# Gate of a graph network: at three steps TensorE folds a product tile alone, and GpSimd's addition is left out

## The reference, cut to what matters

```python
def _gate(h, q, Wg, bg, Wq, bq):           # h: 8 x 32 nodes x 768, q: 8 x 64 x 768
    hg = einsum('bnf,gf->bng', h3, Wg[:, :F])
    qg = einsum('blf,gf->blg', q, Wg[:, F:]) + bg
    attn = sigmoid(hg[:, :, None, :] + qg[:, None, :, :])
    qi = einsum('bnlf,blf->bnf', attn, q)
    alpha = sigmoid(einsum('bnf,gf->bng', h3, Wq[:, :F]) + einsum('bnf,gf->bng', qi, Wq[:, F:]) + bq)
    return (alpha * tanh(qi) + (1.0 - alpha) * h3).reshape(B * N, F)
```

## Time and profile before

| | |
|---|---|
| median of 3 runs | 822.61 us (822.32 to 822.70) |
| profiled execution | 822.72 us, span 820.9 us |
| PE busy | 773.7 us (94%) |
| DVE busy | 606.1 us (74%) |
| POOL busy | 514.2 us (63%) |
| ACT busy | 424.9 us (52%) |
| L590 POOL, first additions | 94 in 223.0 us, mean 2394 ns |
| L1424 PE, identity products | 464 records in 58.9 us |
| L1974 DVE, gate products | 96 in 217.7 us, mean 2279 ns |

### The profile page before, as it was taken

One profiled execution on the slowest core, in us unless ns is written; L12 is line 12 of the kernel. 1 busy time (PEld: TensorE's weight loads), 2 busy tenths in 40 slices (PEclk: granted clock), 3 DMA queues, 4 the chain that ended last, 5 costly groups with the idle time before them and its releaser, 6 DMA issues.

```text
span 820.9 us, 10574 instructions
## 1 busy us (share of the span) xinstructions
PE 773.7 (94%) x4196; PEld 641.8 (78%) x4196; DVE 606.1 (74%) x664; ACT 424.9 (52%) x507; POOL 514.2 (63%) x219
## 2 busy tenths in 40 slices
PE   7999999999988999988888889999999999998998
PEld 4669986776645699667655548999999999975897
DVE  8966239999999641888999996865696488565454
ACT  6524447677674342666676735444443454253742
POOL 0625609999999273499999964870685177805500
PEclk9999999999999999999999999999999999999999
DMA  9037525345332474260063327556356545350001
GB/s 365 31 78 233 163 88 157 86 147 155 115 116 77 123 231 146 67 180 12 26 231 116 108 85 268 194 192 221 103 177 204 181 137 210 116 231 0 2 1 39
DMA packets 24409, 111.01 MB, mean 135 GB/s; under 512 B 3620, under 2 KB 6180, under 8 KB 23976
## 3 DMA queue, kind: packets, MB, share of 16 engines
q1 hardware_dynamic: 23240, 104.24, 39.3%
q10 hardware_dynamic: 1120, 6.10, 1.9%
HBM read 100.63 MB, written 0.79 MB: 124 GB/s over the span
## 4 chain that ended last, share of the span: by engine, by line
PE 58%; POOL 19%; DVE 18%; ACT 3%; issue 2%; DMA 0%; DVEq 0%; ACTq 0%
PE ps L1087 28%; POOL prod L590 13%; DVE prod L1974 11%; PE ps L1118 5%; PE ps L1053 5%; POOL prod L593 4%; DVE qi_t L1992 3%; PE ps L1595 3%; PE ps L1245 2%; PE ps L1266 2%; PE ps L1424 1%; PE ps L1656 1%; PE ps L1246 1%; PE ps L1315 1%; POOL w_lo L578 1%
## 5 line engine op out<-in xcount | busy, mean ns | idle before, releaser
L578 POOL TENSOR_TENSOR w_lo<-w_raw,w_hi 128x1536 fp32r<-128x1536 f32 x49 | 183.8, 3764 | 141.6 <-ACT w_hi L670 141.5
L590 POOL TENSOR_TENSOR prod<-prod 128x1024 f32<-128x1024 f32 x94 | 223.0, 2394 | 45.9 <-DVE prod L1974 45.7
L806 ACT ACTIVATE prod<-ps 128x1024 f32<-128x1024 f32 x192 | 187.3, 1023 | 73.1 <-PE ps L1377 60.9
L1974 DVE TENSOR_TENSOR prod<-prod,ps 128x2048 f32<-128x2048 f32 x96 | 217.7, 2279 | 5.3 <-ACT prod L806 3.6
L670 ACT ACTIVATE w_hi<-w_raw 128x1536 fp32r<-128x1536 f32 x60 | 88.9, 1487 | 119.1 <-PE ps L1087 108.6
L1377 PE MATMUL ps<-sel_pair,h_and_q 128*128 128x512 f32 x384 | 128.6, 447 | 16.7 <-ACT prod L806 16.4
L1087 PE MATMUL ps<-w_hi,yt_hi 128*128 128x384 f32 x480 | 122.9, 336 | 0.0
L1087 PE MATMUL ps<-w_lo,yt_hi 128*128 128x384 f32 x480 | 121.9, 334 | 0.0
L1087 PE MATMUL ps<-w_hi,yt_lo 128*128 128x384 f32 x480 | 121.8, 334 | 0.0
L1377 PEld LDWEIGHTS ps<-sel_pair,h_and_q 128*128 128x128 f32 x384 | 67.1, 190 | 52.0 <-ACT prod L806 31.7
L1053 PE MATMUL ps<-w_raw,h_t 128*128 128x384 f32 x312 | 106.8, 486 | 0.0
(11 more groups left out here) (254 smaller groups left out, 1102.9 us busy)
## 6 DMA issues: line engine op xcount, KB each, us to landing
w_raw<-weights SPq DMA_DIRECT2D x105, 768.0 KB, 4.4
wa_in<-weights SPq DMA_DIRECT2D x6, 768.0 KB, 5.8
w_gat<-weights SPq DMA_DIRECT2D x6, 768.0 KB, 8.0
w_query<-weights SPq DMA_DIRECT2D x3, 768.0 KB, 11.8
h_and_q<-stage_hi SPq DMA_DIRECT2D x24, 96.0 KB, 2.1
h_and_q<-stage_lo SPq DMA_DIRECT2D x24, 96.0 KB, 2.2
a_vec<-gat_vectors ACTq DMA_DIRECT2D x1, 2048.0 KB, 9.6
q_t<-queries ACTq DMA_DIRECT2D x1, 1536.0 KB, 12.7
```

What stands on the lines that cost most here:

```text
L578: pool.tensor_tensor(Wl[:, j, :], raw_slab(U, 0, j), Wh[:, j, :], ALU.subtract).then_inc(w_lo_by_pool, 1)
L590: pool.tensor_tensor(v[:, :, 0:32], v[:, :, 0:32], v[:, :, 32:64], ALU.add).then_inc(folded_once, 1)
L806: act.activation(slot_view(s)[:, :, 32 * u:32 * u + 32], args.rearrange("p b (n l) -> p (b n) l", l=LH), ACT.Sigmoid).then_inc(sigmoid_rea ...
L1974: TT(slot_view(s), slot_view(s), ps[:, 6, o:o + L].unsqueeze(1).broadcast_to([P, NB, L]), ALU.mult).then_inc(products_ready, 1)
```

## The change

A list `WHOLE` names steps 6, 12 and 18 of the second gate, so far of the kind "tensor". There TensorE takes all 64 queries in sixteen identity products, not eight after GpSimd's addition; it waits for VectorE's product alone, and GpSimd passes the step over. ScalarE, which reuses the slot four steps later, waits for the fold of that step in place of the addition, for both halves. The counts that other waits use are adapted. The steps at which folds and reductions stand are the same.

```diff
+WHOLE = [(), (6, 12, 18)]
 def kind_of(i, s):
+    if s in WHOLE[i]:
+        return "whole"
     if s + 3 in FOLD_AT[i]:
         return "tensor"
...
             def fold(i, s):                       # GpSimd
+                if KIND[i][s] == "whole":
+                    return
...
                     if s >= PSLOTS:               # ScalarE, sigmoid
-                        if u == 1:
-                            act.wait_ge(folded_once, (STEPS - 1) * i + (s - PSLOTS + 1))
-                        elif KIND[i][s - PSLOTS] == "tensor":
-                            act.wait_ge(fold_ready, count_kind(i, s - PSLOTS, "tensor"))
+                        if u == 1 and KIND[i][s - PSLOTS] != "whole":
+                            act.wait_ge(folded_once, by_pool(i, s - PSLOTS))
+                        elif KIND[i][s - PSLOTS] in ("tensor", "whole"):
+                            act.wait_ge(fold_ready, by_tensor(i, s - PSLOTS))
...
                     bank7_free(at_)               # TensorE, fold
-                    pe.wait_ge(folded_once, (STEPS - 1) * i + (s + 1))
+                    n = 8
+                    if KIND[i][s] == "whole":
+                        pe.wait_ge(products_ready, STEPS * i + (s + 1))
+                        n = 16
+                    else:
+                        pe.wait_ge(folded_once, by_pool(i, s))
                     o = ps[:, 7, 0:4 * NB].rearrange("p (n l) -> p n l", l=4)
-                    for k in range(8):
-                        mm = pe.matmul(o, ident[:], slot_view(s)[:, :, 4 * k:4 * k + 4], start=(k == 0), stop=(k == 7))
+                    for k in range(n):
+                        mm = pe.matmul(o, ident[:], slot_view(s)[:, :, 4 * k:4 * k + 4], start=(k == 0), stop=(k == n - 1))
```

More of the change, by code:

```diff
@@ L79 @@
 KIND = [[kind_of(i, s) for s in range(STEPS - 1)] for i in range(2)]
-REST_AT = [[s + (3 if KIND[i][s] == "tensor" and KIND[i][s + 1] != "tensor" else 2) for s in range(STEPS - 1)] for i in range(2)]
+REST_AT = [[s + (3 if s + 3 in FOLD_AT[i] and s + 4 not in FOLD_AT[i] else 2) for s in range(STEPS - 1)] for i in range(2)]
 QUERY_EVENTS = [0, 1, 5, 6]
@@ L426, in count_kind, with by_tensor, by_pool @@
             return sum(k == kind for g in range(i) for k in KIND[g]) + sum(k == kind for k in KIND[i][:s + 1])
+        def by_tensor(i, s):
+            return count_kind(i, s, "tensor") + count_kind(i, s, "whole")
+        def by_pool(i, s):
+            return (STEPS - 1) * i + s + 1 - count_kind(i, s, "whole")
         def head_views(g):
@@ L591, in fold @@
                 if KIND[i][s] == "pool":
-                    pool.wait_ge(folded_once, (STEPS - 1) * i + (s + 1))
+                    pool.wait_ge(folded_once, by_pool(i, s))
                     pool.tensor_tensor(v[:, :, 0:16], v[:, :, 0:16], v[:, :, 16:32], ALU.add).then_inc(folded_twice, 1)
@@ L1982, in reduce @@
                         terms = slot_view(s)
-                    elif KIND[i][s] == "tensor":
-                        dve.wait_ge(fold_ready, count_kind(i, s, "tensor"))
+                    elif KIND[i][s] in ("tensor", "whole"):
+                        dve.wait_ge(fold_ready, by_tensor(i, s))
                         terms = ps[:, 7, 0:4 * NB].rearrange("p (n l) -> p n l", l=4)
@@ L1989, in reduce @@
                     else:
-                        dve.wait_ge(folded_once, (STEPS - 1) * i + (s + 1))
+                        dve.wait_ge(folded_once, by_pool(i, s))
                         terms = slot_view(s)[:, :, 0:32]
```

## The result

The changed kernel takes 826.32 us (median of 5, 825.78 to 826.78) against 822.61 us before (median of 5, 821.41 to 822.70): ratio 1.0042, 95% interval 1.0030 to 1.0053, 3.7 us more. The forecast was 824.5 us. The direction was right, the size short by 1.8 us: the measured time lies outside the forecast's own band (823.7 to 825.3), near rival (a) with its 826.2, at the very end of the whole range (826.3), which had been drawn so as to take that rival in. Two more jobs gave 826.39 against 822.30 us (1.0048, 1.0032 to 1.0063) and 825.46 against 822.58 us (1.0036, 1.0022 to 1.0049).

The account below looks back on a forecast made before the run. It took the gate's chain to run over GpSimd's additions and TensorE's folds, then VectorE. Three fold extensions of 1.79 us, less 1.82 slack and 1.62 clock loss, gave +1.93: 824.5 us on the medians' scale, range 822.3 to 826.3.

Parts of the forecast that it names:

- rival (a): TensorE's clock falls as before or inside a longer fold, so 1.62 us aren't regained: 826.2 us, chance 0.18.
- What bounds the gate: Second gate: chain passes GpSimd, TensorE, ScalarE, then VectorE; any delay reaching the product at 416.10 reaches the end whole.
- Prices: Durations read from the trace; sixteen more records lengthen each of three TensorE folds by 1.79 us.
- Carried forward: Delays followed engine by engine through steps 6, 12 and 18 of the second gate, ending 1.93 us late.
- Removed: Three first additions of GpSimd, 7.0 us, go; GpSimd waits for products instead, and no VectorE speedup is booked.
- The clock: TensorE's half-clock stretch at 376.0 to 379.4 us was expected to vanish with shorter thin stretches: -1.62 us.
- Rival (b): Comes out even: delays absorbed by GpSimd's later additions, or records follow more closely; 822.6 us, chance 0.20.
- X: Time that 16 more records add to each longer TensorE fold, taken as 1.79 us.
- Rival (c): Faster: added products lie in TensorE's idle time before folds, -2.5 us, 820.1 us, chance 0.12.

Follow-up runs that it names:

- e6: Kernel before with eight more identity products, to spare columns, at TensorE's steps 9, 15 and 21; GpSimd keeps its three additions: 826.08 us, ratio 1.0050.
- e1: The kernel before run once more with no edit: 821.72 us over 12 executions, ratio 0.9995.
- e3: Kernel before with only step 12 folded whole by TensorE: 824.20 us, ratio 1.0017.
- e4: Kernel before with only step 18 folded whole by TensorE: 823.43 us, ratio 1.0010.
- e12: Kernel before with VectorE's last reduction of the second gate done twice, so everything behind the gate comes later: 824.53 us against 822.88, ratio 1.0032.
- e8: Changed kernel with twelve identity products instead of sixteen at the three steps, a quarter of their terms left out: 823.24 us, ratio 1.0012.
- e7: Changed kernel with eight identity products instead of sixteen at the three steps, the upper 32 queries left out: 821.25 us, ratio 0.9992.

## Why the prediction was right, and where it was short

**What bounds the gate.** Right. The chain goes through TensorE at the folds, and what reaches product 27 reaches the end: product 27 to 47 takes 64.3 to 64.4 us in every trace.

**Prices.** Right: 3.73 us for 32 records (3.74), 3.49 from the fold to the next arguments.

**Carried forward.** Right step by step, for two profiles of which one has the fall. Forecast and measured starts: product 10 at 367.65 and 367.61, the fold of 11 at 376.2 and 376.21, product 16 at 385.71 and 385.69, the fold of 18 at 397.05 and 397.09, the fold of 20 at 403.86 and 403.89, product 27 1.93 and 1.92 late. Counted from product 0, the measured starts are 0.09 later than these, which still leaves all within 0.15 us.

**Removed.** "I book nothing" for VectorE was right: its products took 2.28 us in this stage in the kernel before and in the changed one. And e6 shows that with the longer folds GpSimd's relief is worth nothing at all.

**The clock.** This step failed. It took the fall at 376 us in the one profile as part of the kernel before and booked its end as a gain of 1.62 us, because the thin stretches get shorter. The fall did stay away in four traces with the longer folds at all three steps (the three of the changed kernel and e6), but it comes and goes in the kernel before as well: of the traces with its order up to step 14 of TensorE three have it (before, e1, e3) and two don't (e4, e12), e12 behind the very same thin stretch. That the longer folds keep the fall away is not shown. At equal clock the gate of the kernel before takes 78.34 us, and the change costs 81.44 - 78.34 = 3.1 us instead of 1.9. The fall was also mis-sized where it counts: it takes 79.43 - 78.34 = 1.1 us of product 27, not the 1.62 that TensorE's own path lost, because without the fall TensorE's fold of 14 waits for GpSimd instead (e12). At equal clock the forecast's own sum is 1.93 + 1.62 = 3.55 us, and less those 0.5 us it is 3.0, beside the 3.1 measured. On the scale of executions without a costly fall the gate's 3.1 us give 821.0 + 3.1 = 824.1, against 823.96 and 824.18 for the fastest measured.

**Rival (a)** gave 826.2, and the median was 826.3. Its words were that the 1.62 us aren't regained, by a fall as before or inside a longer fold. Neither was seen: of four traces of the longer folds at all three steps none has a fall between 336 and 430 us, three have one at 751 us, which cost 1.4 us in the first profile. That the median fell on this rival's number, and with it still inside the range, is luck: what it gave as its reason was not seen.

**Rival (b)** needed X of 1.15 or less: measured 1.78. Nor would 1.15 have been even at equal clock: e8, with X at 0.89, already costs 0.65 us, and a straight line between e7 and e8 puts the zero near 0.6 (an estimate). **Rival (c)** is e7: with X = 0 the gain is 1.2 us at equal clock, while the forecast's 2.5 contained the end of the fall.

**Open.** At equal clock the change costs 3.1 us; the medians of the three jobs differ by 3.7, 4.1 and 2.9. What makes up the rest isn't settled; the time ahead of product 0, which varies by 1.2 us, and falls near 751 us both have a part in single executions. Whether the changed kernel meets more falls of the clock, as its 16 executions suggest, or drew a few more by chance, the runs don't settle; a mere delay of what follows (e12) did not bring them.

## What to carry to other kernels

Taking work from an engine that is nearly always busy need not help much, even if nothing is paid for it: the 7.0 us taken from GpSimd were worth 1.2 us with no work added (e7) and nothing beside the longer folds (e6). And it costs if the receiving engine has no idle time at that very place: TensorE waited 3.5 us for GpSimd in this stage, but the three folds that grew had no idle time behind them before the next arguments, and 3.1 of the 3 x 1.78 = 5.3 us came out at product 27. Lay the new instruction into the timeline and carry the delay engine by engine; here that gave every start within 0.15 us. And before a difference of a few tenths of a per cent is read from two profiles, count the falls of TensorE's clock in each and compare stretches at equal clock.

## What the runs showed of the hardware

The time of one and the same kernel goes with the mean granted clock of TensorE, loosely: 821.1 us at 0.999 to 1.0, 822.7 at 0.997, 824.9 at 0.992 in the 12 executions of e1, but 820.7 to 823.6 at 0.997 in 36 others. Single stretches of 3.4 us at 0.50 begin at a few places, 251, 376, 431 to 433, 448 to 451 and 748 to 752 us, in some executions and not in others. The same 3.9 us with 11 matmul records were followed by one in the kernel before and by none in e12. What one costs depends on who sets the pace: 1.1 us at 376, 1.4 at 751, nothing between 431 and 451, where the chain runs over VectorE.
